# Products that nobody reads: TensorE work added to a two-layer attention and expert kernel, behind the first sequence's units and in twelve slots between the experts

## The reference

```python
x = x + _L0_attn_ref(_layernorm(x), Wq, Wk, Wv, Wo)      # causal, 16 heads of 8, softmax
x = x + _L0_ffn_ref(_layernorm(x), ...)                  # 8 experts, the best 2 per token, 128 -> 512 -> 128, relu
x = x + _L1_attn_ref(_layernorm(x), wq, wk, wv, wo)      # linear: energy = K^T V, context = Q energy
x = x + _L1_ffn_ref(_layernorm(x), ...)                  # 8 experts, the best 1 per token
```

## Time and profile before

| | |
|---|---|
| median of 3 runs | 625.31 us (624.05 to 626.15) |
| the profiled execution's own time | 627.74 us |
| its span | 626.0 us |
| TensorE busy (products) | 525.9 us, 84% |
| VectorE busy | 463.8 us, 74% |
| ScalarE busy | 353.5 us, 56% |
| GpSimd busy | 338.7 us, 54% |
| mean granted TensorE clock | 0.911 |

### The profile page before, as it was taken

The page is one execution under the profiler, slowest core; times in us unless marked ns, Lnnn a source line. Parts: engine busy times, 40 slices in busy tenths (PEclk is TensorE's granted clock), DMA queues, the critical chain, the costliest instruction groups (busy, mean ns, idle before and its releaser), DMA issues.

```text
span 626.0 us, 15238 instructions
## 1 busy us (share of the span) xinstructions
PE 525.9 (84%) x4916; PEld 441.7 (71%) x4931; DVE 463.8 (74%) x1320; ACT 353.5 (56%) x958; POOL 338.7 (54%) x459
## 2 busy tenths in 40 slices
PE   3079999999889999897579999999896574889995
PEld 2036666677667666665379999999896563879995
DVE  5466777977998798877388796554898887787662
ACT  2014555755475556553356686664875756656663
POOL 2104444444456661665775777777854744455555
PEclk9657999999999997997779999999898866699999
DMA  6664444444445544414542333222773312544320
GB/s 165 118 132 96 101 108 104 104 103 105 103 107 108 131 107 88 101 45 162 199 103 63 98 100 94 82 83 82 213 287 90 100 54 85 134 150 143 100 74 17
DMA packets 59532, 69.45 MB, mean 111 GB/s; under 512 B 9241, under 2 KB 50657, under 8 KB 57148
## 3 DMA queue, kind: packets, MB, share of 16 engines
q1 hardware_dynamic: 51744, 53.01, 33.7%
q0 software_dynamic: 7168, 14.77, 7.0%
q10 hardware_dynamic: 540, 0.69, 0.6%
HBM read 45.31 MB, written 23.67 MB: 110 GB/s over the span
## 4 chain that ended last, share of the span: by engine, by line
PE 34%; DVE 4%; DMA 3%; issue 3%; ACT 2%; SPq 2%; POOL 2%; DVEq 0%; POOLq 0%; ACTq 0%
PE h_ps_e L1861 15%; PE y_ps_e L1873 14%; PE xT_ps_e L1849 2%; DMA xt_e<-expert_queues 1%; PE h_ps_e L1930 1%; SPq L1360 1%; POOL expert_rows L1280 1%; POOL expert_queues L1132 1%; PE h_ps_e L1925 1%; ACT rxr L1767 1%; ACT L1720 1%; SPq L1345 0%; PE l_ps_e L1945 0%; DMA back_e<-expert_rows 0%; SPq L1361 0%
## 5 line engine op out<-in xcount | busy, mean ns | idle before, releaser
L617 DVE TENSOR_REDUCE mx<-max_ps 128x2 f32<-128x512 f32 (+1 forms) x192 | 128.5, 688 | 49.5 <-PE max_ps L277 47.5
L1705 ACT ACTIVATE hT_e<-h_ps_e,wb_e 128x128 f32<-128x128 f32 x448 | 121.9, 387 | 28.3 <-PE h_ps_e L1861 26.4
L1861 PE MATMUL h_ps_e<-xT_e,wb_e 128*128 128x128 f32 x896 | 116.0, 285 | 1.9 <-ACT hT_e L1705 1.0
L1861 PEld LDWEIGHTS h_ps_e<-xT_e,wb_e 128*128 128x128 f32 x896 | 110.7, 201 | 3.3 <-ACT xT_e L1696 1.7
L1873 PE MATMUL y_ps_e<-wb_e,hT_e 128*128 128x128 f32 x896 | 109.3, 275 | 3.1 <-DVE yt_e L1430 3.1
L1873 PEld LDWEIGHTS y_ps_e<-wb_e,hT_e 128*128 128x128 f32 x896 | 104.5, 192 | 3.3 <-DVE yt_e L1430 3.3
L457 ACT ACTIVATE pT<-sc_ps 128x1024 f32<-128x1024 f32 x64 | 65.7, 1027 | 70.0 <-PE sc_ps L305 69.8
L1280 POOL DMA_INDIRECT expert_rows<-yt_e,go_e x72 | 77.9, 1082 | 32.4 <-issue 18.0
L863 POOL TENSOR_TENSOR turn<-eps 128x1 f32<-128x1 f32 x64 | 13.2, 206 | 144.4 <-ACT pT L457 144.0
L1417 DVE COPY wb_e<-wpack 128x1156 f32 x112 | 82.4, 778 | 8.4 <-issue 4.9
L58 POOL DMA_INDIRECT expert_queues<-rxr,rseats x64 | 66.7, 1042 | 19.5 <-issue 17.0
(11 more groups left out here) (284 smaller groups left out, 968.8 us busy)
## 6 DMA issues: line engine op xcount, KB each, us to landing
wpack<-in_wpack SPq DMA_DIRECT2D x2, 4112.0 KB, 15.0
parts_scratch<-parts SPq DMA_DIRECT2D x16, 384.0 KB, 3.5
xt_e<-expert_queues SPq DMA_DIRECT2D x40, 129.0 KB
xt_e<-expert_queues SPq DMA_DIRECT2D x72, 64.5 KB
wpack<-parts_scratch SPq DMA_DIRECT2D x24, 192.0 KB
kst<-parts_scratch SPq DMA_DIRECT2D x24, 192.0 KB
qst<-parts_scratch SPq DMA_DIRECT2D x72, 64.0 KB
wpack<-parts_scratch SPq DMA_DIRECT2D x63, 64.0 KB
```

The lines of the kernel that those rows point to most:

```text
L617: nc.vector.reduce_max(mx[:, s, h0:h0 + n], max_ps[:, (k + 1) % 2, :].rearrange("p (h k) -> p h k", h=n), axis=AX.X).then_inc(unit_reduced, 1)
L1705: last = nc.scalar.activation(hT[i % 2][:, s, c, :], h_ps[h_bank(i)][:, s, c * RT:(c + 1) * RT], ACT.Relu, bias=wb[i % 4][:, s, FF + c:FF ...
L1861: last = nc.tensor.matmul(h_ps[h_bank(i)][:, s, c * RT:(c + 1) * RT], wb[i % 4][:, s, c * P:(c + 1) * P], xT[i % 2][:, s * RT:(s + 1) * RT ...
```

## The change

Two functions named `keep_awake` are added to TensorE's program. They issue products whose results are read by nobody, into banks that are free at that time, with operands that are always there (the identity, and a constant triangle). They wait for nothing and signal nothing. One stands behind each of the twelve units of the first sequence, with three more behind the last (128 columns, f32). In slots 5 to 16 one stands behind the second product and two behind the outputs (256 columns, f32). No other engine's program changes.

```diff
+            def keep_awake(n):
+
+                for _ in range(n):
+                    nc.tensor.matmul(av_ps[:, 0:P], ident[:], ident[:], start=True, stop=True)
...
                 for k in range(NU):
                     unit(0, 0, k)
+                    keep_awake(1)
+                keep_awake(3)
                 transpose_max(0)
...
+            def keep_awake(n):
+
+                for _ in range(n):
+                    nc.tensor.matmul(h_ps[0][:, 0, 0:S], ident[:], t["tri"][:], start=True, stop=True)
+
+            def slot_begin(i, awake=0):
                 if i < NSEQ:
                     turn(i)
                 if 0 <= i - 1 < NSEQ:
                     second_product(i - 1)
-
-            def slot_end(i):
+                keep_awake(awake)
+
+            def slot_end(i, awake=0):
                 if i < NSEQ:
                     first_product(i)
                 if 0 <= i - 1 < NSEQ:
                     outputs(i - 1)
+                keep_awake(awake)
                 for g in choices(i - 1):
                     rank(g)
...
             for i in range(NI1 + 1 - SLOT, SLOTS - 3):
-                slot_begin(i)
-                slot_end(i)
+                slot_begin(i, 1)
+                slot_end(i, 2)
```

More of the change, by code:

```diff
@@ L1961, in rank @@
                 last.then_inc(ranked, 1)
-            def slot_begin(i):
+            def keep_awake(n):
+                for _ in range(n):
+                    nc.tensor.matmul(h_ps[0][:, 0, 0:S], ident[:], t["tri"][:], start=True, stop=True)
+            def slot_begin(i, awake=0):
                 if i < NSEQ:
```

## The result

The change takes 620.84 us (median of 7 executions, 618.76 to 624.51) against 625.45 us of the kernel before (7, 624.05 to 628.01): ratio 0.9941, 95% interval 0.9919 to 0.9962 (the two medians alone give 0.9926).

A forecast was written before the change was run, and what follows sets the result against it. TensorE at its lower clock was taken to bound the first body, a VectorE, ScalarE and TensorE relay the slots, GpSimd's sends their end. Terms 0.3 - 0.3 + 0.6 - 0.9 = -0.3 us gave 625.0, stated as 624.9; range 622.2 to 627.2.

The forecast's parts named there:

- Price of a product: TensorE time per added product: 0.43 us (128 columns) or 0.85 (256) at the lower clock, half at the upper.
- Term A: First sequence's units: products cost 1.1 us, then the clock rises by units three to six and returns 0.8; +0.3 us.
- Term B: Body 0: the clock falls again near 47 us and it runs as now, except its first four units; -0.3 us.
- rival 1: The clock stays up through body 0, 2.6 us off, 622.4 us; chance 0.27.
- The sign that I had named for being wrong: The time before 62 us moves by over 1.5 us, or extra products leave ScalarE waiting between outputs and turning.
- Term C: Slots 6 to 8: exposed extra products delay VectorE's sum of slot 8; +0.6 us, between -0.1 and +1.1.
- Rival 2: Slots 7 and 8 run at the lower clock and their products stand in the way; +2.5, 627.5 us; chance 0.14.
- Term D: Slots 11 to 13: the clock stays up, so GpSimd's third group starts earlier; -0.9 us.
- Everything behind 532 us is as before: Second layer: TensorE starts it after a pause with the clock down, as before; no change in time.
- Rival 3: The clock doesn't rise in the first sequence's units; +2.9, 627.9 us; chance 0.06.
- rival 4: The products do nothing to the clock and lie in waits; 625.3 to 626.2 us; chance 0.08.

The follow-up runs named there:

- units_only: Only the 15 products of the first sequence's units, none in the slots, against the kernel before: 624.24 us, ratio 0.9958.
- both_c: The change unaltered, timed once more against the kernel before: 624.40 us, ratio 0.9984; its profiled execution took 619.46 us.
- body0: The change plus one product behind each of body 0's first four units and four before its first scores: 620.83 us, ratio 0.9893 to the kernel before.
- before_again: The kernel before, unaltered, against itself for a second profile: ratio 0.9994.
- late_slots: Products in slots 10 to 16 alone, none in the units or slots 5 to 9, against the kernel before: 624.31 us, ratio 0.9996.
- slots_only: Only the 36 products of slots 5 to 16, none in the units, against the kernel before: 625.41 us, ratio 0.9981.
- both_again: The change unaltered, run again for a second profile and more timings, against the kernel before: 623.79 us, ratio 0.9952.
- eight_rows: The change with every added product over 8 rows instead of 128, against the kernel before: 652.64 us, ratio 1.0457.
- before_p2: The kernel before, unaltered, one execution for a third profile: 624.96 us.

## Why the prediction was wrong, by its own steps

**Price of a product.** 0.43 us at the lower clock was forecast for 128 columns. In the units such a product takes 34.14 - 33.61 = 0.53 from its start to the next; the first four units take 5.50 us with their products (31.41 to 36.91) against 3.62 (32.14 to 35.76), which is 0.47 for each. Part of the miss is that I read a unit from the one that takes 0.85, while the four take 0.91 on average. The rest may be that the products stand between bf16 ones here and between f32 ones in the earlier trace rows; no run parts that. For 256 columns 0.85 was right (1.71 for two).

**Term A, +0.3.** The rise came in the fifth unit (37.8 us), inside the forecast's third to sixth; from the first unit (31.41) to the maxima (43.93) it is 12.52 us against 11.79 from 32.14: +0.7, inside the bounds of -0.5 to +0.9. Over all profiles the maxima come at 44.09 instead of 43.66. Right in mechanism, small in size; and in the profile of units_only a quicker finish was lost in the wait for the next stack.

**Term B, -0.3, is the step that failed.** "I take it that it falls again near 47 us and that body 0 then runs as now": true of the profiled execution (48.0 us) and of three of five profiles. In the other two it stays up. I had set forecast and rival 1 against each other as two possible kernels; they are two executions of one. Rival 1's price was right: 14.2 - 11.6 = 2.6 forecast, 62.26 - 59.30 = 3.0 measured in both_c, and in body0 the upper heap goes when eight products fill the thin stretch in front of the first scores. The sign that I had named for being wrong, a move of over 1.5 us before 62 us, is there in both_c and not in the first profile. Its chance of 0.27 was of the wrong thing: it should have been a share of the executions (12 in 28), and the median of a few executions falls wherever that share puts it: 620.84, 623.79 and 624.40 in three comparisons. That the first caught five of seven in the lower heap is luck of the draw: beside its own kernel before, the third has 624.40 against 624.66, which is what I had forecast.

**Term C, +0.6.** Slot 6 did run at the lower clock, as forecast, and the sum of slot 8 came as late as I had it. It stands here, behind slot 5's turning in the changed kernel and, as the last row, the same turning in the kernel before (its sum is the 489.85 of the earlier trace rows):

```profile
470.56 0.41 PE L1930 MATMUL h_ps_e<-ident,xn_e 128*128 128x128 f32 x2
...
486.68 0.66 PE L1952 MATMUL l_ps_e<-m_e,xnT_e 128*128 128x144 f32 x4
...
487.38 0.42 DVE L1531 TENSOR_TENSOR rxr<-l_ps_e,x 128x256 f32<-128x256 f32 x1 [0.67 <-PE l_ps_e L1952]
```

```profile
473.58 0.41 PE L1923 MATMUL h_ps_e<-ident,xn_e 128*128 128x128 f32 x2
```

487.38 - 470.56 = 16.82 us against 489.85 - 473.58 = 16.27: 0.55 us late. The two other profiles of the change in which the clock falls near 478 us have 16.82 and 16.78, the two in which it doesn't 16.24 and 16.23. Of the kernel before, three have 16.07 to 16.29; before_again has 17.61, with the clock down from 477.5 to 487.8 us. late_slots, with the fall and without products there, has 15.97. One profile doesn't fit: slots_only, with products and no fall, has 16.59. What the sum missed lies behind: the step to the next slot's sum takes 5.0 us in the change and 5.25 in the three, and at row 1 the delay is 0.3 (34.73 against their 34.41). No run says what gives it back. So term C was +0.3 where slot 6 runs at the lower clock and -0.2 where it doesn't; my bounds were +1.1 and -0.1. Rival 2 (+2.5) did not happen in any profile.

**Term D, -0.9**, is exact: 17.41 to 16.54 us; all profiles with full-height products in the late slots have it and none without them.

**What the sum left out.** "Everything behind 532 us is as before" missed 0.45 us of the second layer (93.38 to 92.93). The profile of both_c is 4.5 us below the mean of the three of the upper heap, 2.8 of them up to the transposes behind body 0; the rest lies in several stages, at most 0.8 us each either way, with the clock's falls in other places. That of both_again is 3.4 us below, and only 0.8 of them are there by then, since its clock rose late in the units and took back what body 0 gave; 1.2 lie between tile 0 and slot 5. So body 0 is what was seen to differ between the heaps, and 1.7 to 2.6 us of their distance are in stages that no run isolated; that part stays open. Put together from the profiles (means, against the four of before):

| | up to the transposes (A, B) | bodies 1-15 | slot 5 to row 1 (C) | rows 1-14 (D) | second layer | span |
|---|---|---|---|---|---|---|
| forecast | 0.0 | 0 | +0.6 | -0.9 | 0 | -0.3 |
| upper heap, 3 profiles | -0.7 | -0.6 | +0.1 | -0.9 | -0.4 | -2.2 |
| lower heap, 2 profiles | -2.5 | -1.1 | -0.5 | -0.9 | -0.6 | -6.2 |

The stages left out hold the rest, and before_again raises the mean of before in column C by 0.25. By the medians of the executions the heaps are 1.2 and 5.9 us below the kernel before.

**The range** (622.2 to 627.2) was drawn around 0.45 of a wrong pair of alternatives. It stopped at rival 1 (622.4), in which C still stood at +0.6 and the second layer at nothing. Rival 3 (no rise in the units) did not happen, nor rival 4.

## What to carry to other kernels

Where a clock stays up or falls by a margin that the program hardly sets, the time is not one number but two, and a change moves executions between them: look at several profiles of one kernel before you price a difference, and count executions. Products that nobody reads paid here where TensorE bounds the work behind a pause that it would spend idle anyway; over 8 rows they cost 27 us. The version with most of them (618.0 and 618.9 us, ratio 0.990 to 0.991 to the kernel before) has all its executions in one heap, but by its interval it is not parted from the change with body 0's eight (0.9893, 0.9864 to 0.9923): what the two tiles add is seen in the profiles and not in the ratios. What is saved in front of a transfer can be lost to it.

## What the runs showed of the hardware that was not expected

- A product over 8 rows costs more than the same over 128. Both at the lower clock, one of 128 f32 columns in a unit takes 33.82 - 33.09 = 0.73 us to the next start, against 34.14 - 33.61 = 0.53; one of 256 takes 1.00 us against 0.85. The Trainium skill, page "TensorE: Matmul & The Clock Gate", section "Why this matters for your kernels", has a product of 32 rows take as long as one of 128. No run here has 32 rows; at 8 rows of f32 operands the product was not as short as at 128 but longer.
- In eight_rows TensorE's clock stood at 0.50 for 78.5 us on end (490.4 to 568.9) with TensorE busy 77.1 of them, most of it in slots with products over 8 rows, the last 10 us in tiles without any.
- A granted clock of 1.00 in a window is no proof. In eight_rows the units read 1.00, though the four products of a unit last 0.63 us as at the lower clock (0.39 at the upper). The kernel before has the same in before_p2: 1.00 in 45.0 to 54.1 us, while its four first-score products take 1.06 us, as in the profile of the earlier trace rows at 0.50. The window of eight_rows:

```profile
32.10:42.40 10.30, 10.25 (x41) 5.80 (x41) 4.15 (x6) 0.00 (x0) 0.00 (x0) 1.00 0.69 153
```

The Trainium skill, section "Seeing it yourself" of the same page, calls the clock's trace events unreliable on trn2; here the durations of the products were the better witness.
